# A fused decoder kernel on one core: stores, row orders of the first turns, and transposes in pairs

## The reference, cut to what matters

```
# 1: attention over a memory of 8192 neurons
xB = x @ Bm ; h = scan(h @ A + u)           # over the 256 tokens
importance = softmax(x . (h_final @ W_imp.T))
token_pref = softmax(x @ W_router.T)        # 64 neurons
neuron_w   = normalised importance @ token_pref
shared_compress = einsum('bn,ndr->bdr', neuron_w, compress)   # 256x128 for each batch
Q      = x @ shared_compress ;  scores = Q @ K.T / sqrt(128)  # 256 x 8192 for each batch
top 8 of each row, softmax ;  output = weights @ V[topk_idx]
x1 = layernorm(x + output)
# 2: cross attention, 16 heads of 64
q = x1 @ Wq ; k, v = ctx @ Wkv ; sim clipped to [-5, 5] ; softmax ; out @ Wo + bo
x2 = layernorm(x1 + ...)
# 3: experts: in each group of 32 tokens every expert set takes its best token
x3 = layernorm(x2 + expert output put back to the tokens)
```

## Time and profile before

| | |
|---|---|
| median of 3 runs | 1380.46 us (1378.34 to 1381.36) |
| the profiled execution | 1377.7 us |
| its span in the trace | 1375.8 us |
| TensorE busy | 1321.6 us, 96% of the span |
| VectorE busy | 1125.4 us, 82% |
| ScalarE busy | 718.8 us, 52% |
| GpSimd busy | 728.9 us, 53% |

### The profile page before, as it was taken

How to read it: one execution, slowest core, us unless ns; L and a number is a source line. 1 busy time by engine, 2 the same in 40 slices (tenths; PEclk the granted TensorE clock), 3 DMA queues, 4 the chain that set the end, 5 groups by cost and what they waited for, 6 DMA issues and landing times.

```text
span 1375.8 us, 25304 instructions
## 1 busy us (share of the span) xinstructions
PE 1321.6 (96%) x9877; PEld 993.5 (72%) x9877; DVE 1125.4 (82%) x1628; ACT 718.8 (52%) x1377; POOL 728.9 (53%) x1009
## 2 busy tenths in 40 slices
PE   9877999999999999999999999999999999999898
PEld 5455778786878787878787868787878676767775
DVE  2479889898989898989898988898989986546567
ACT  1353655555555555555555555555555544336554
POOL 0554465555565656565655565656565647341434
PEclk9997999999999999999999999999999999999999
DMA  9562121212121212121212121212121216002412
GB/s 368 182 197 65 46 74 54 74 55 74 54 74 55 74 54 74 55 74 54 74 54 74 54 74 54 74 55 74 54 74 44 74 42 182 1 26 84 156 43 83
DMA packets 57557, 110.38 MB, mean 80 GB/s; under 512 B 9446, under 2 KB 38110, under 8 KB 56286
## 3 DMA queue, kind: packets, MB, share of 16 engines
q1 hardware_dynamic: 40350, 62.17, 15.0%
q0 software_dynamic: 14848, 41.96, 10.6%
q10 hardware_dynamic: 2240, 4.63, 0.9%
HBM read 98.50 MB, written 10.22 MB: 79 GB/s over the span
## 4 chain that ended last, share of the span: by engine, by line
PE 88%; DVE 5%; issue 2%; another core or an unknown queue 2%; ACT 2%; DMA 0%; SPq 0%; POOL 0%; POOLq 0%; ACTq 0%; DVEq 0%
PE side_bank L387 51%; PE score_bank L387 33%; PE score_bank L766 2%; DVE cand_idx L1177 1%; DVE cand_val L1174 1%; PE side_bank L766 1%; DVE dispatchedT L1335 1%; PE side_bank L548 1%; ACT exp L922 0%; PE score_bank L606 0%; ACT score_row L910 0%; SPq L318 0%; DVE x_sum L1200 0%; POOL exp L1425 0%
## 5 line engine op out<-in xcount | busy, mean ns | idle before, releaser
L910 ACT COPY score_row<-score_bank 128x512 f32<-128x512 f32 x512 | 298.9, 591 | 112.2 <-PE score_bank L387 56.7
L1397 POOL DMA_INDIRECT v_rows<-in_V,top_idx x256 | 249.0, 973 | 130.8 <-issue 74.5
L1174 DVE MAX8 cand_val<-score_row 128x8 f32<-128x2048 f32 x128 | 291.7, 2279 | 28.6 <-ACT score_row L910 26.3
L1177 DVE FIND_INDEX8 cand_idx<-cand_val,score_row 128x8 uint32<-128x2048 f32 x128 | 292.5, 2285 | 0.0
L1425 POOL TENSOR_SCALAR exp<-exp,exp_bound 128x256 f32<-128x256 f32 x512 | 248.9, 502 | 79.8 <-ACT exp L922 78.1
L387 PE MATMUL score_bank<-keysT_hi,qT_hi 128*128 128x512 f32 x512 | 216.9, 424 | 21.0 <-ACT score_row L910 19.9
L387 PE MATMUL score_bank<-keysT_hi,qT_lo 128*128 128x512 f32 x512 | 204.9, 400 | 0.0
L387 PE MATMUL score_bank<-keysT_lo,qT_hi 128*128 128x512 f32 x512 | 204.7, 400 | 0.0
L922 ACT ACTIVATE exp<-side_bank 128x512 f32<-128x512 f32 x256 | 139.1, 595 | 91.3 <-PE side_bank L387 84.3
L387 PE MATMUL side_bank<-qT_heads,kT 64*128 64x256 f32 x1024 | 145.2, 402 | 2.6 <-ACT exp L922 2.6
L387 PEld LDWEIGHTS score_bank<-keysT_hi,qT_hi 128*128 128x128 f32 x512 | 97.9, 191 | 62.1 <-ACT score_row L910 25.3
(11 more groups left out here) (200 smaller groups left out, 2284.0 us busy)
## 6 DMA issues: line engine op xcount, KB each, us to landing
kT<-den_scratch SPq DMA_DIRECT2D x62, 256.0 KB
f_quads<-in_f POOLq DMA_DIRECT2D x32, 256.0 KB, 3.4
comp_then_wqkv_raw<-in_comp SPq DMA_DIRECT2D x6, 1024.0 KB, 19.0
xT_by_step<-in_xTs SPq DMA_DIRECT2D x4, 1024.0 KB, 9.1
xT_in<-in_xT SPq DMA_DIRECT2D x16, 256.0 KB
keysT_raw<-in_KmT ACTq DMA_DIRECT2D x8, 512.0 KB, 20.2
x_sum<-in_x SPq DMA_DIRECT2D x32, 128.0 KB, 2.0
ctxT_in<-in_ctxT SPq DMA_DIRECT2D x16, 256.0 KB
```

The costliest lines, as they stand in the source:

```text
L910: nc.scalar.copy(srow[n // PER % 2][:, i * CB:(i + 1) * CB], scb[n % 3]).then_inc(sem("score_evac"), 1)
L1174: own(nc.vector.max(cv[:, tile, cs], srow[g % 2][:, :]))
L1177: nc.vector.max_index(ci[:, tile, cs], cv[:, tile, cs], srow[g % 2][:, :]).then_inc(sem("cand_done"), 1)
L1397: pool.indirect_dma_start(out=vg[:, k, :], out_offset=None, in_=V_rows, in_offset=bass.IndirectOffsetOnAxis(ap=i8[:, tile, k:k + 1], axis=0))\
```

## The change

**First stage.** `router(0)` moves from behind `power(4)` to before `power(2)`, `router(1)` to behind `power(3)`, both in front of the Bm products. `router(2)` and the transposes of quarters 2 and 3 move too. VectorE does both `token_weights` back to back behind the reductions of all four quarters, with ScalarE's exponentials in the same order. The unread products behind the importance product are five instead of three, those behind the compress products 22 instead of 16.

**Stores.** Before, each block of 32 rows was stored in two pieces, the 2 rows of batch 0 and the other 30: eight stores for the first half of the columns, four small ones for the second half, then the read of batch 0, then four of 30 rows. Now the first half is stored in four pieces of 32 rows. When the second half is there, batch 0's rows go out in two stores, each of one row from all four blocks; then the read, then the other rows of the second half.

**First turns.** TensorE and ScalarE do turn -1 and the first part of turn 0 from functions `ramp()` with an order written out. The values of batch 0 stand between rows g7 and g8, its keys between g8 and g11, and 17 unread products (`fill`) in two groups around the second transpose of x1. On VectorE the first half of `x1_lo` stands before the maxima of g10, and the value sum and the normalisation of tile 1 between those maxima and their indices. In turn 0 the value sum of batch 1 comes behind row g15 instead of before it, and `rstd1` behind all heads.

**Last stage.** Transposes and collects come in twos.

The diff, cut to its core:

```diff
-        jobs += [("K", c, j) for j in range(4)]
+        jobs += [("K", c, j) for j in range(2 if c == 0 else 0, 4)]
+    if c == -1:
+        jobs += [("K", 0, j) for j in range(2)]
...
-            for half in range(2):
-                sp.wait_ge(sem("sc_act"), 2 * half + 2)
-                sp.wait_ge(sem("sc_dve"), 2 * half + 2)
-                store_rows(half, 0, KT, "sc0_stored")
-                if half == 0:
-                    store_rows(0, KT, B * KT, "sc_stored")
-            sp.wait_ge(sem("sc0_stored"), 16 * 8)
+            sp.wait_ge(sem("sc_act"), 2)
+            sp.wait_ge(sem("sc_dve"), 2)
+            store_rows(0, 0, "sc0_stored")
+            sp.wait_ge(sem("sc_act"), 4)
+            sp.wait_ge(sem("sc_dve"), 4)
+            for k in range(KT):
+                sp.dma_start(scd_b0[k], scs[k:P:32, CH:2 * CH]).then_inc(sem("sc0_stored"), 16)
+            sp.wait_ge(sem("sc0_stored"), 16 * 6)
             sp.dma_start(sct[:, :, :], scd_v[0]).then_inc(sem("sct_in"), 16)
...
-            for r in range(4):
-                power(r)
-                if r < 3:
-                    warm(1, pp[0])
+            power(0)
+            warm(1, pp[0])
+            power(1)
+            pe.wait_ge(sem("small_in"), 16 * 5)
+            pe.wait_ge(sem("xs_in0"), 16)
+            router(0)
+            power(2)
+            warm(1, pp[0])
+            power(3)
+            pe.wait_ge(sem("xs_in1"), 16)
+            router(1)
...
-            warm(16, pp[1])
+            warm(22, pp[1])
...
+            def fill(n):
+                job_free(pe, ("Q", 0, 0))
+                for _ in range(n):
+                    mm(job_bank(("Q", 0, 0))[:, 0:P], idn[:, :], idn[:, :])
+            def ramp():
+                for e in range(12):
+                    score(-1, e)
+                shared_q(1)
+                for e in range(12, 20):
+                    score(-1, e)
+                need(pe, "ctx_lo", 1)
+                need(pe, "w_lo", len(WCHUNKS))
+                project_v(0, 0)
+                project_v(0, 1)
+                for e in range(20, 24):
+                    score(-1, e)
+                project_v(0, 2)
+                project_v(0, 3)
+                project(("K", 0, 0), 1, 0, cth, ctl)
+                for e in range(24, 28):
+                    score(-1, e)
+                project(("K", 0, 1), 1, 2 * P, cth, ctl)
+                for e in range(28, 32):
+                    score(-1, e)
+                x1_transpose(0, 0)
+                for e in range(4):
+                    score(0, e)
+                project(("K", 0, 2), 1, 4 * P, cth, ctl)
+                project(("K", 0, 3), 1, 6 * P, cth, ctl)
+                fill(10)
+                x1_transpose(0, 1)
+                fill(7)
+                need(pe, "x1_lo", TT)
+                for j in range(2):
+                    project(("Q", 0, j), 0, 2 * j * P, x1h, x1l)
+                for e in range(4, 8):
+                    score(0, e)
+                project(("Q", 0, 2), 0, 4 * P, x1h, x1l)
+                sims(0, 0)
+                project(("Q", 0, 3), 0, 6 * P, x1h, x1l)
+                for e in range(8, 12):
+                    score(0, e)
...
-            for n in range(-2, NT):
-                if n + 2 < NT:
-                    inter_transpose(n + 2)
-                if n >= 0:
-                    collect(n)
+            for n in range(-2, NT, 2):
+                for i in range(2):
+                    if n + 2 < NT:
+                        inter_transpose(n + 2 + i)
+                for i in range(2):
+                    if n >= 0:
+                        collect(n + i)
...
+            def first_sum():
+                value_sum(0, 1, range(TOPK))
+                value_norm(0, 1)
...
                 select(c, (0,))
-                if cross:
+                if cross and c:
                     value_sum(c, 1, range(TOPK))
                     x1_lo(c, 0)
                     value_norm(c, 1)
-                candidates(c, 0, 0 if c == 0 else None)
+                candidates(c, 0)
...
-                if mid:
+                if mid and c:
                     value_sum(m, 0, range(TOPK))
                 candidates(c, 4)
+                if c == 0:
+                    value_sum(m, 0, range(TOPK))
...
-                candidates(c, 7)
+                if c == -1:
+                    x1_lo(m, 0)
+                candidates(c, 7, first_sum if c == -1 else None)
+                if c == -1:
+                    x1_lo(m, 1)
...
-                    if mid and h == 9:
+                    if mid and h == 9 and c != 0:
                         rstd1(m, 0)
+                if c == 0:
+                    rstd1(m, 0)
```

More of the change, by code:

```diff
@@ L1175, in candidates @@
                 if between is not None:
-                    x1_lo(between, 1)
+                    between()
                 nc.vector.max_index(ci[:, tile, cs], cv[:, tile, cs], srow[g % 2][:, :]).then_inc(sem("cand_done"), 1)
```

193 lines of the change are left out of this document (124 added, 69 removed).

## The result

In 9 runs of each kernel, taken in turns on one chip, the changed kernel took 1371.61 us (1367.73 to 1375.13) and the one before 1378.34 us (1375.56 to 1381.36). The ratio is 0.9950, with a 95% interval of 0.9935 to 0.9965: 6.9 us faster, between 4.8 and 9.0. Forecast were 8.0 us and a time from 1368 to 1378. The span of the profiled execution is 1369.8 us.

The account below looks back on a forecast made before the run. TensorE, with 88% of the chain, bounds the full middle; VectorE bounds the ramp. First stage 2.3, stores 1.6, ramp 0.6 and last stage 3.5 sum to 8.0 us: 1372.4 us beside the median, range 1368 to 1378.

Parts of the forecast that it names:

- first stage: Up to the compress products: router products moved and both diagonals ready early bring these 2.3 us forward, bounds 0 and 3.5.
- stores: Compress products to SyncE's read of batch 0: fewer small stores bring the read 1.6 us forward, bounds 0.6 and 2.0.
- read to second row's maxima: The 3.9 us lead at batch 0's read reaches the second row's maxima whole, at 78.6 us; nothing added.
- ramp, to shared_q: Until TensorE is full: queries start at 146.4 instead of 151.28, shared_q 0.7 us earlier; value 0.6, bounds -2.0 and +2.0.
- shared_q to fourth reciprocal: Turn 0: tile 0's variance and normalisation and row 16's maxima come some 2 us later, at no cost.
- last stage: Pairs of transposes and collects: two tiles take 3.16 us instead of 3.46; gain 3.5 us, bounds -0.7 and 4.0.
- If the clock rises behind it: First stage, after product 0: TensorE then runs at full clock and the scan starts at 21.3 us, 0.4 earlier.
- the first stage gives nothing: Rival: product 0 waits longer or the clock stays low until the Bm products; 5.7 us gained, 1374.8; chance 0.17.
- Data is late next: Second row's maxima: they wait for Wv's data, so six extra unread products behind the compress products add nothing.
- The rival that TensorE would bound the ramp at half clock: Ramp: values, keys and four rows of scores take 45 us at the lower level, 21.1 lost, 1393.6; chance 0.04.
- free at the upper level: Ramp: the 17 unread products lie in waits for x1 and cost nothing at full clock.
- The signs of being wrong: VectorE idle between rows 8 and 10, TensorE's clock below 0.8 from 105 to 130 us, late ramp cast, or pair's period 3.4.

Follow-up runs that it names:

- run 2: The changed kernel with the last stage as before, that is everything but the pairs: ratio 0.9982 to the kernel before, 2.5 us faster.
- run 3: The changed kernel with routers, powers and Bm products of the first stage as before: ratio 0.9945 to the kernel before.
- run 4: The changed kernel again, unaltered, for a second trace on another chip: ratio 0.9948 to the kernel before, 7.1 us faster.
- Run 7: The changed kernel with 16 unread products behind the compress products instead of 22: ratio 0.9950 to the kernel before.
- run 6: The changed kernel with the first turns in their old order, without unread products among them: ratio 0.9952 to the kernel before.
- run 10: The changed kernel without the 17 unread products in the ramp: ratio 0.9964 to the kernel before.
- run 11: The changed kernel with three scores moved ahead of the first unread products, into the wait for x1: ratio 0.9951 to the kernel before.
- run 1: The kernel before with only the last stage's transposes and collects in pairs: ratio 0.9962 to the kernel before, 5.2 us faster.
- run 5: The kernel before again, unaltered, for a trace on the chip of the follow-ups: 1371.39 us.
- run 8: The changed kernel with SyncE's two loads of Wv ahead of the last four stores of shared_compress: ratio 0.9934 to the kernel before, 9.1 us faster.

## Why the prediction was right, point by point

The total was 8.0 us, and 6.9 were measured; the sign, the range and the largest term were right, but the first stage and the ramp were not. That the total is so near is in part luck: every mark up to the ramp came later than forecast (compress products 52.7 and not 51.7, read 64.8 and not 63.3, second row 80.3 and not 78.6, shared_q 157.2 and not 155.0), and three terms of the table came out higher than forecast (from the read to the second row, behind shared_q, and the last stage). The measured terms are means over the traces of one kind.

| term | forecast | measured |
|---|---|---|
| first stage | 2.3 | 0.6 |
| stores | 1.6 | 1.1 |
| read to second row's maxima | 0 | 0.7 |
| ramp, to shared_q | 0.6 | -0.5 |
| shared_q to fourth reciprocal | 0 | 0.5 |
| last stage | 3.5 | 4.15 |
| sum | 8.0 | 6.5 |

The ramp's row has the four traces with the old order (76.35 us) against those of runs 2, 3, 4 and 7 and the trace after (76.87). With the spreads of the first and the fourth row, the sum of 6.5 is no surer than to some 1 us, and the 6.9 lies within that.

**First stage.** The step that failed is "If the clock rises behind it". In four of ten traces it doesn't, and the scan starts at 24.3 to 24.8, beyond the forecast's own bound of 1.9 us late; in the six others it does, but then product 1 (run 4) or the last product (five traces) pays half clock once more. The work taken out was counted right (2.12 us against 1.9). Product 0 waited for its quarter of x and not for the identity, and ran at 8.56 where 9.0 was forecast. The rival "the first stage gives nothing" is closer than the sum (run 3). Ahead of the slow last product TensorE was not idle: from 33.1 to 35.9 us it is busy 2.5 of 2.8 us, most of it with 32 products of 16 columns; the same work stands there in run 2, where the clock does not fall. Why the clock rises early in some traces and late in others, and why it then falls at one product, was not tried and is open.

**Stores.** The mechanism is right. The last store began at 61.36, 0.83 us behind VectorE's last copy and not 0.63, for the first of the two took 0.71 us to issue; and it took 3.39 us and not 3.14. In all eleven traces with the new stores it is 12.03 to 12.08 us from the compress products to the read, against 13.06 to 13.22 with the old ones.

**The lead at the second row.** "Data is late next" was right in the trace after, and the place too, Wv's cast: it begins at 76.42 and not at 79.02, 2.6 us earlier, with a lead of 2.4 at the read. Only the size of the lead came from the terms ahead. It is not right in every trace: in runs 6, 7, 10 and 11 the second row follows the first at once, and so it did before (82.50 is 4.61 us behind 77.89), where the first row was as much a bound as the cast. The 0.7 us in the table are the difference of two means, 15.8 us from the read to the second row with the old stores (15.3 to 16.0) and 15.0 (14.3 to 15.5) with the new. They may be the unread products', which the forecast had at nothing: with 22 the first row starts 9.5 us behind the read on the average, with 16 it is 11.0. Run 7, with 16 and 15.2 us, speaks against it; the cause is open.

**Ramp.** The queries came 5.1 us earlier against the second row's maxima (63.7 us behind them instead of 68.8; in runs 1 and 5 the old order has 67.2), forecast were 4.9; from them to shared_q 13.2 us, forecast 12.5. The forecast's reason for the small gain fits: six scores, 4.2 us, stand behind the start of the queries, and run 11 takes a part of that out again. (By the code the second half of the values stands behind g8 and the last two keys behind g11.) What the term missed is that its base, the old order, was itself 1.55 us long by the clock at the values in the trace of before; in run 5 it is not. The rival that TensorE would bound the ramp at half clock was wrong: 0.91 from 120 to 130 us. The unread products were more than free, without them it is 2.3 us longer to shared_q (run 10). The forecast took them as "free at the upper level", with no gain. Its own figures gave 0.7 us (159.62 - 158.9), and the sum has 0.6. Up to the fourth reciprocal the 0.46 us behind shared_q come in addition (run 6), which the forecast had at no cost and no gain.

**Last stage.** Right, 0.65 us more than forecast. A pair takes 3.12 us and not 3.16, over 14 pairs 0.56. The forecast took 1.00 us for the second tile of transposes where its own row gave 1.06, and the pair is shorter all the same. The end behind the last transposes grew by the forecast's 1.4 us (9.58 against 8.19 in the traces).

**The middle and the signs.** Right: where the turns are even, they are so in both kernels, 957.00 us in run 5 and 957.07 in run 4, from the fourth to the last reciprocal. The signs of being wrong that the trace after can be read for did not come: VectorE is busy 24.3 of the 25 us from 105 to 130 us, TensorE's clock is 0.91 there, and the pair's period is 3.12 us.

## What to carry to other kernels

A lead is worth what the next late thing leaves of it: name that thing with its issue time, not only its landing, since a load that stands behind four stores in one queue can be moved ahead of them, which is cheaper than moving the work before it; and look what stands right behind the thing that you move (here the first row, run 8). Work brought forward into idle time gains little if as much other work is pushed behind the point from which the engine is full. Where the clock of TensorE changes by trace, compare stretches between marks over several traces: one trace of before put 1.5 us into this ramp that the code doesn't own, and a gain that goes with the clock, as in run 11, is not yet the gain of the edit.

## What was not expected of the hardware

- The records of TensorE last twice as long at the start of the trace although the granted clock reads 1.00. The Bm products in the earlier trace rows took 3.39 us for eight records, while the table of stretches of the kernel before has 1.00 there:

```profile
15.00:18.00 3.00, 2.73 (x7) 1.30 (x9) 0.13 (x1) 0.61 (x2) 0.00 (x0) 1.00 1.06 415
```

  Before the first change that is recorded, the clock column can't be read; the length of a record can.
- One kernel took 1371.6 us on one chip and 1364.8 on another, and the traces put most of it into the turns (run 4).
- Unread products around a wait of 4 us shorten the time at half clock but don't rule it out: without them it lasts from 140.3 to 150.5 us (15.85 us from the first query product to shared_q), with them from 141.9 to 145.3 in the trace after (13.20 us), and in run 8 the clock is 1.00 there throughout (12.65 us).
- From the last reciprocal to the last stage it took 90.5 or 90.6 us in the four traces with the old order of the first turns, and 89.9 to 91.8 us in the ten with the new, the same kernel having 89.87 and 91.48. No run was aimed at it.
